# GpSimd adds up the residual between the scatters of two pairs, with x loaded in eight pieces ahead of the loop

## What is computed

```
xn = _layernorm(x)                       # x: (8, 1024, 128) = 64 tiles of 128 tokens
out = x + mamba2(xn) + moe(xn)           # mamba2(xn) itself returns xn + y @ W_out.T

# mamba2: y is scaled row by row with rsqrt(mean(y*y) + eps) ahead of W_out
# moe: the two best of 8 experts for each token, weights w from a softmax
h   = silu(xn @ gate[e]) * (xn @ up[e])  # 128 -> 256
moe = sum over the token's two experts of w * (h @ down[e])
```

## Time and profile before

| | us |
|---|---|
| median of 3 runs | 794.11 (792.69 to 797.33) |
| the profiled execution's own time | 795.79 |
| its span, first to last instruction | 794.0 |
| PE busy | 631.2 (79%) |
| DVE busy | 585.2 (74%) |
| ACT busy | 462.3 (58%) |
| POOL busy | 400.4 (50%) |
| first scatter to `moe_d` starts | 520.12 |
| first final load is issued | 760.32 |

### The profile page before, as it was taken

The page is one execution under the profiler, slowest core; times in us unless marked ns, Lnnn a source line. Parts: engine busy times, 40 slices in busy tenths (PEclk is TensorE's granted clock), DMA queues, the critical chain, the costliest instruction groups (busy, mean ns, idle before and its releaser), DMA issues. The chain is left out here.

```text
span 794.0 us, 15139 instructions
## 1 busy us (share of the span) xinstructions
PE 631.2 (79%) x3701; PEld 531.9 (67%) x3703; DVE 585.2 (74%) x1410; ACT 462.3 (58%) x1014; POOL 400.4 (50%) x601
## 2 busy tenths in 40 slices
PE   0695629998999989999998998699898889988700
PEld 0695317777778777778777776587777777777600
DVE  7787898898898888888898888555565555654445
ACT  0352446688777878877788775454555555554400
POOL 3000006576766766766676767145555555555510
PEclk9999999799999999999999999799999999999955
DMA  9950100000000000000000015133333333333169
GB/s 306 266 130 0 29 1 23 19 27 23 29 22 22 28 22 22 28 22 22 25 26 22 29 24 184 36 88 99 97 85 96 88 98 98 85 98 86 54 252 382
DMA packets 64647, 61.43 MB, mean 77 GB/s; under 512 B 9242, under 2 KB 55710, under 8 KB 64624
## 3 DMA queue, kind: packets, MB, share of 16 engines
q1 hardware_dynamic: 56176, 44.11, 19.7%
q0 software_dynamic: 8448, 17.06, 6.2%
HBM read 30.19 MB, written 31.47 MB: 78 GB/s over the span
## 5 line engine op out<-in xcount | busy, mean ns | idle before, releaser
L449 POOL DMA_INDIRECT moe_d<-raw,slot_st x136 | 133.8, 984 | 124.6 <-issue 102.1
L422 POOL DMA_INDIRECT slots_d<-rows,slot_st x128 | 134.6, 1052 | 73.8 <-POOL rows L417 52.5
L1040 DVE SCALAR_TENSOR_TENSOR act<-raw,taps,act 128x512 f32<-128x512 f32 x192 | 149.3, 785 | 23.9 <-ACT act L513 23.1
L398 POOL TENSOR_TENSOR xde<-xb,e_end 128x256 f32<-128x256 f32 x64 | 45.6, 713 | 113.2 <-DVE xb L1117 111.6
L1233 DVE CAST x_hi<-bank 128x256 fp32r<-128x256 f32 x68 | 28.8, 424 | 95.4 <-PE bank L871 91.8
L864 PE MATMUL bank<-xw_hi,x_hi 128*128 x136 | 61.1, 449 | 27.2 <-DVE x_lo L1235 22.7
L774 PE MATMUL bank<-xb,m_sb 128*128 128x64 f32 x512 | 75.9, 298 | 3.8 <-POOL xde L398 3.8
L774 PEld LDWEIGHTS bank<-xb,m_sb 128*128 128x128 f32 x512 | 73.1, 216 | 5.6 <-issue 3.9
L890 PE MATMUL bank<-act,raw 128*128 x544 | 72.0, 275 | 1.8 <-issue 1.8
L664 ACT ACTIVATE raw<-bank 128x256 f32<-128x256 f32 x68 | 26.5, 391 | 77.2 <-remote 68.5
L890 PEld LDWEIGHTS bank<-act,raw 128*128 128x128 f32 x544 | 66.1, 192 | 1.9 <-issue 1.9
(11 more groups left out here) (231 smaller groups left out, 1659.4 us busy)
## 6 DMA issues: line engine op xcount, KB each, us to landing
slots_d<-rows SPq DMA_DIRECT2D x8, 1122.0 KB, 13.4
rows<-slots_d SPq DMA_DIRECT2D x68, 132.0 KB
x_sb<-in_x SPq DMA_DIRECT2D x8, 512.0 KB, 7.0
act<-in_x SPq DMA_DIRECT2D x64, 64.0 KB
xw_hi<-moe_d SPq DMA_DIRECT2D x8, 512.0 KB, 9.3
xw_lo<-moe_d SPq DMA_DIRECT2D x8, 512.0 KB, 9.9
out<-x_sb SPq DMA_DIRECT2D x8, 512.0 KB, 13.5
moe_d<-raw,slot_st POOLq DMA_INDIRECT x136
```

What stands on the lines that cost most here:

```text
L398: nc.gpsimd.tensor_tensor(by_head(xde[:, u, :]), by_head(xdt[:, u, :]), per_head(e_end, nn), ALU.mult).then_inc(xde_done, 1)
L422: nc.gpsimd.indirect_dma_start(out=slots_d, out_offset=bass.IndirectOffsetOnAxis(ap=slot_st[:, r, c:c + 1], axis=0), in_=rows[:, r, c, :], ...
L449: nc.gpsimd.indirect_dma_start(out=moe_d, out_offset=bass.IndirectOffsetOnAxis(ap=slot_st[:, r, c:c + 1], axis=0), in_=ym[r][:, c * D:(c + ...
L1040: V.scalar_tensor_tensor(out=group_act(par)[:, t, :], in0=proj[:, t, k:k + GT], scalar=taps[:, t, k:k + 1], in1=group_act(par)[:, t, :], o ...
```

## The change

An internal HBM tensor `x_d` is added, and SP copies x to it (4 MB, HBM to HBM) behind the writes that clear `slots_d`. The eight x loads go from `x_d` to `x_again`, which now is a region of `xw_lo` (64 tiles, 4 MB), behind the first weights. So the low part of the gate and up weights moves to the second half of `xw_hi`. The 64 loads of the pair loop are gone. ACT reads `x_again[:, t]` and writes `x_norm[r]`, which has the place of the old `x_again[r]`. The multiply-add of DVE becomes a multiply and an add on POOL, behind the two scatters of its step, and a semaphore `resid_added` takes the place of `place_free`.

```
-        gu_hi, gu_lo = xw_hi[:, 0:E * 2 * F], xw_lo[:, 0:E * 2 * F]
+        gu_hi, gu_lo = xw_hi[:, 0:E * 2 * F], xw_hi[:, E * 2 * F:2 * E * 2 * F]
-        x_again = [act[:, 3072 + r * D:3072 + (r + 1) * D] for r in range(R)]
+        x_again = xw_lo[:, 0:NT * D].bitcast(F32).rearrange("p (t d) -> p t d", d=D)
+        x_norm = [act[:, 3072 + r * D:3072 + (r + 1) * D] for r in range(R)]
...
@@ sync
+            sp.dma_start(x_d, x).then_inc(st_x, 16)
             sp.wait_ge(csp_done, 4)
...
             gate_up_load(raw[:, 0:3072], 0, 6, ld_moe_w)
+            sp.wait_ge(st_x, 16)
+            sp.wait_ge(proj_done, NG * NAT)
+            for i in range(8):
+                sp.dma_start(x_again[:, 8 * i:8 * i + 8, :], x_d[:, 8 * i:8 * i + 8, :]).then_inc(ld_again, 16)
             sp.wait_ge(gate_done, NT - GC)
             gate_up_load(act[:, 0:1024], 6, 2, ld_moe_w2)
...
-            def load_again(m, r):
-                sp.wait_ge(place_free, m * R + r + 1)
-                sp.dma_start(x_again[r], x[:, tile_ix(m * R + r), :].rearrange("p a d -> p (a d)"))\
-                    .then_inc(ld_again[r], 16)
-            sp.sem_inc(place_free, R)
-            over_pairs(sp, [(slot_load, 0)], [load_again])
+            over_pairs(sp, [(slot_load, 0)])
+            sp.wait_ge(resid_added, NT)
...
@@ gpsimd
+            def residual(m, r):
+                t = tile_ix(m * R + r)
+                xt = x_sb[:, t, :].rearrange("p a d -> p (a d)")
+                pool.wait_ge(rms_done, 1)
+                pool.wait_ge(resid_done, m * R + r + 1)
+                pool.sem_inc(scatters, 1)
+                nc.gpsimd.tensor_tensor(xt, xt, var[:, t].broadcast_to([P, D]), ALU.mult).then_inc(resid_scaled, 1)
+                pool.wait_ge(resid_scaled, m * R + r + 1)
+                pool.sem_inc(scatters, 1)
+                nc.gpsimd.tensor_tensor(xt, xt, x_norm[r], ALU.add)\
+                    .then_inc(resid_added, 1)
-            over_pairs(pool, [(moe_scatter, 0)])
+            over_pairs(pool, [(moe_scatter, 0)], [residual])
...
@@ scalar
                 act_e.wait_ge(rms_done, 1)
-                act_e.wait_ge(ld_again[r], 16 * (m + 1))
+                act_e.wait_ge(ld_again, 16 * 8)
                 t = tile_ix(m * R + r)
-                A(x_again[r], x_again[r], ACT.Identity, bias=nmr1[:, t], scale=r12[:, t]).then_inc(resid_done, 1)
+                if not is_first(m):
+                    act_e.wait_ge(resid_added, (m - 1) * R + r + 1)
+                A(x_norm[r], x_again[:, t, :].rearrange("p a d -> p (a d)"), ACT.Identity, bias=nmr1[:, t],
+                  scale=r12[:, t]).then_inc(resid_done, 1)
...
@@ vector
-            def residual(m, r):
-                dve.wait_ge(resid_done, m * R + r + 1)
-                t = tile_ix(m * R + r)
-                xt = x_sb[:, t, :].rearrange("p a d -> p (a d)")
-                V.scalar_tensor_tensor(out=xt, in0=xt, scalar=var[:, t], in1=x_again[r], op0=ALU.mult, op1=ALU.add)\
-                    .then_inc(place_free, 1)
-            over_pairs(dve, [(x_keep, 0), (destination, 2), (hidden, 1)], [residual])
+            over_pairs(dve, [(x_keep, 0), (destination, 2), (hidden, 1)])
-            dve.wait_ge(place_free, NT + R)
+            dve.wait_ge(resid_added, NT)
```

More of the change, by code:

```diff
@@ L77, in program @@
         ncs_d = nc.dram_tensor("ncs_d", (2 * NH, NT, P), F32, kind="Internal").ap()
+        x_d = nc.dram_tensor("x_d", (P, NT, D), F32, kind="Internal").ap()
         x_sb = sb("x_sb", [P, NT, D])
@@ L174, in program @@
             "ld_w", "ld_moe_w", "ld_moe_w2", "st_zero", "st_cs", "st_out"))
-        scatters = sem("scatters")
+        scatters, st_x = sem("scatters"), sem("st_x")
         ld_x = [sem(f"ld_x{i}") for i in range(8)]
@@ L180, in program @@
         st_moe = [sem(f"st_moe{i}") for i in range(R)]
-        ld_again = [sem(f"ld_again{i}") for i in range(R)]
+        ld_again = sem("ld_again")
         ld_sum = [[sem(f"ld_sum{i}_{c}") for c in range(K)] for i in range(8)]
@@ L208, in program @@
         gu_hi_done, gu_lo_done, xhi_done = sem("gu_hi_done"), sem("gu_lo_done"), sem("xhi_done")
-        ms_done, rms_sq, rms_done, resid_done, place_free, total_done = (sem(n) for n in (
-            "ms_done", "rms_sq", "rms_done", "resid_done", "place_free", "total_done"))
+        ms_done, rms_sq, rms_done, resid_done, resid_added, total_done = (sem(n) for n in (
+            "ms_done", "rms_sq", "rms_done", "resid_done", "resid_added", "total_done"))
+        resid_scaled = sem("resid_scaled")
         def by_head(t):
```

## The result

| | before | changed |
|---|---|---|
| median, us | 795.01 (792.69 to 797.33, 4 runs) | 907.51 (903.7 to 908.14, 4 runs) |
| ratio | | 1.139, 95% interval 1.136 to 1.143 |
| profiled execution's own time / span | 795.79 / 794.0 | 908.12 / 906.4 |
| first scatter starts | 520.12 | 525.81 |
| scatter of pair 4 | 535.15 | 540.12 |

The rows of before in the second half of the table are those of the earlier trace rows and of the table ahead. The span grew by 112.4 us: 5.0 up to pair 4, 103.2 from pair 4 to pair 63, 4.2 from there to the last scatter, nothing behind it.

What follows compares the result with a forecast made beforehand. PE alone is not the limit; POOL's groups of four scatters and late `y_keep` repeat, 3.53 us a step. The new wait's ring adds 94 us, the loads 2: 892 from the profiled 795.79, so 890 as median, range 868 to 922.

Steps and rivals of the forecast that it cites:

- the ring: Pair loop: `y_keep`, scatters, multiply, add and ACT's residual run one after another, 5.08 us a step against 3.53; +94.1 us.
- the two POOL operations: POOL's multiply and add behind each pair's scatters: 0.38 us each, bounds 0.30 and 0.60.
- ACT's idle time: Pair loop: ACT idle 2.5 to 3 us before its residual in each step, released by POOL's add.
- The tail: Pairs 65 to 67, where ACT has no residual: they follow as fast as POOL can, 3.67 us each.
- rival 2: Pair loop: the ring does not bind, POOL's own work does; 3.67 us a step, 804 us; chance 0.06.
- the 0.83: Pair loop: part of the time from the add's start to the next scatter, taken as 1.23 less `y_keep`'s own time.
- The copy: Before the pair loop: copying x to `x_d` costs 0 to 10 us, taken as 0.
- The +2 for the loads: Before the pair loop: x loads delay the last weights, ACT waits 0 to 5 us, taken as +2.
- Rival 3: Pair loop: POOL operations break up four scatters holding `y_keep` back; no slower or faster, 782 to 784 us; chance 0.04.
- the hold on `y_keep`: Pair loop before the change: `y_keep` starts only 0.99 us after the last of four scatters; what holds it not shown.

Runs made afterwards that it cites:

- e1: Changed kernel with eight `x_norm` places in place of four, so ACT waits for the add eight tiles back: 827.83 us against 792.25 before (1.046).
- e3: Changed kernel with POOL's multiply and add put ahead of the scatters of each step, four places kept: 818.86 us against 792.25 before (1.034).
- The doses: Changed kernel without POOL's multiply (866.04 and 864.42 us) or with its add done twice (942.25 us); one execution each.
- e7: Changed kernel with POOL's multiply by the row factor left out: 866.04 us in one execution, where the kernel before takes 765.15.
- e12: Kernel before plus one unused 128x128 POOL add behind each step's two scatters, on a slow-kind chip: 798.05 us against 795.89 (1.001).
- e4: Kernel before plus a one-column POOL memset that nobody reads, behind each step's two scatters: 795.63 us against 792.25 (1.010).
- e5: Kernel before plus one unused 128x128 POOL add behind each step's two scatters, on the fast chip: 767.43 us against 765.15 (1.000).
- e6: Changed kernel with the fused multiply-add back on DVE and the eight x loads behind the last weight loads: 766.49 us against 765.15 before (1.0006).
- e10: Same kernel as e5 (kernel before plus an unused 128x128 POOL add), run again on the fast chip: 766.11 us against 764.86 (1.001).
- e9: The changed kernel itself, run again where the kernel before takes 764.86 us: 904.45 us (1.180).
- e2: Changed kernel with the fused multiply-add back on DVE, which frees the place; copy, loads and moved weights stay: 795.35 us against 792.25 before (1.004).

## Why the prediction was right, point by point

**The forecast** of 890 (868 to 922) named the ring, and the ring is what happened; the measured 907.51 lies in the range and 17.5 over the value.

**The ring.** e1 and e3 remove it, one by more places and one by the order of the queue, and with it 77 and 86 of the 112 us, each against the kernel before of its own group. The doses move the step by what they add or take. That is shown. Its terms, against the earlier trace rows:

| term | predicted | measured in the rows above |
|---|---|---|
| `y_keep` to first scatter | 1.23 | 1.20 |
| two scatters, to the multiply | 2.27 + 0.02 | 610.82 - 608.53 = 2.29 |
| multiply | 0.38 | 0.44 |
| multiply to add | 0.17 | 0.19 |
| add | 0.38 | 0.46 |
| add to ACT's residual | 0.25 | 612.16 - 611.91 = 0.25 |
| residual to `y_keep` | 0.38 | 0.40 |
| sum | 5.08 | 5.23 |

The term that was mis-sized is the two POOL operations, 0.14 of the 0.15 us: halving the variable part of the 0.60 us of the earlier trace rows gave 0.38, and they take 0.44 and 0.46. The rule of the Trainium skill (GPSIMD Engine Reference, section 4.1) that such work takes GpSimd about twice as long as VectorE would have made each 0.69; the trace has 1.3 times the 0.347 us of the earlier trace rows for each, and two operations stand in place of one fused. So the rule was too high here for one operation. ACT's idle time, which I gave as 2.5 to 3 us, is 3.44: it is the 5.23 of the ring less the 1.79 from the residual at 606.93 to the end of ACT's last copy at 608.72, and I had not worked it out.

**Where the 17.5 us are.** 60 x (5.23 - 5.08) = 9.0. The first step of a turn takes 0.13 more, 14 times: 1.8. One step, from pair 56 to 57, takes 7.07 in place of 5.24: 1.8. The second scatter of pair 56 starts 3.14 us behind the first, where it is at most 1.32 in all other pairs, and this is so in all 14 profiles, that of before among them. No term of the forecast had it, and its cause is open. Up to pair 4 it was 5.0, not 2.0: 3.0. The tail has 3.81 a step and not 3.67, 0.4. Sum 16.0. Of the 1.5 that are left about 1.1 is how the two profiled executions stand to their medians (1.7 above in the prediction, 0.6 here).

**The tail.** 3.67 was the sum for a step bound by POOL alone, in the tail and in rival 2. It is 3.82, and again the two operations are what was too small: multiply 0.43, add 0.45 to 0.46. From the end of the add to the next scatter it is 0.45 us in the tail, exactly the 0.83 less 0.38 of the prediction. That was luck in part: the 0.83 came from a step in which the scatter waits for `y_keep`, while in e7 and e12 it follows its one operation after 0.17.

**The front.** The copy cost nothing: the issue to `cs_d` that the earlier trace rows has at 84.76 now starts at 84.59. The +2 for the loads was about right as a mean. The first scatter starts at 520.3 to 525.8, mean 523.5, in the eight profiles with the loads ahead of the weights, and at 520.1 to 522.3, mean 521.2, in the six others (before, e4, e5, e6, e10, e12). The mechanism I gave for it, weights that land late, is only part: ACT waits 1.1 to 1.4 us for them ahead of its last conversion in six of the eight and in none of the six others, but in the changed kernel's first profile and in e3 it doesn't wait at all. In the first profile of the changed kernel, the one of the result, TensorE's granted clock is down to 0.74 while the loads run; in e9, the same program, it stays at 1.00 there, and the first scatter comes 4.9 us earlier (525.81 and 520.89):

```profile
470.00:490.00 20.00, 18.83 (x100) 15.87 (x98) 13.99 (x35) 11.44 (x25) 13.40 (x26) 0.74 0.74 277
```

The columns are as above, and this is the same window of e9:

```profile
470.00:490.00 20.00, 17.71 (x121) 14.89 (x120) 17.69 (x38) 13.11 (x29) 15.44 (x27) 1.00 0.78 284
```

Both have issued the first weights at nearly the same time (474.83 and 474.50), so the two executions part behind that. The last 1.8 us of the 4.9 come behind the first gate product, which starts at 512.34 and 509.19. Here is the changed kernel's first profile and then e9:

```profile
508.00:525.00 17.00, 12.54 (x48) 9.52 (x48) 6.82 (x19) 6.71 (x14) 0.00 (x0) 0.60 0.08 20
...
508.00:525.00 17.00, 14.13 (x78) 11.77 (x79) 8.49 (x25) 7.14 (x18) 2.97 (x3) 0.88 0.13 33
```

So one and the same program differs by 4.9 us in this place, and the slower execution has the lower clock. That doesn't make the 5.0 us the clock alone. In e1 the clock is 1.00 from 470 to 490 and the first scatter still comes at 525.38. And a clock below 1.00 from 470 to 490 is seen only in two of the eight profiles with the loads ahead of the weights (here and in e3, 0.66), in none of the six others, so the loads may have a part in it. How the 5.0 us divide is open.

**PE.** It waits 2.07 us ahead of L899 in the step shown, as forecast, but 1.4 us as a mean of all steps: (215 - 157.48) us over the 41 steps of the window. Its clock did fall, to a mean of 0.90, so that in some steps its work takes longer (the down products above 1.44 us and not 1.06). It did not reach the ring: the sum of the ring's terms, in which no PE instruction stands, is the whole step.

**Rival 2** (bound by POOL, 804) is what e1 and e3 made; it costs more than the 804 said, by the 3.82 for 3.67 and the time that the front takes. **Rival 3** (POOL's work breaks the hold on `y_keep`) is refuted by e12: an operation stands between the pairs and the hold stays. The prediction left open what the hold is, and that stays open. It is not the 64 loads (e2), an operation of 0.43 us between the pairs does not end it (e12), and it is not in the program alone, since the same program has it in some groups and not in others. The ring of the changed kernel does not contain it, hence nearly the same 904 and 908 us in both kinds. It shows only before the ring begins: from the first scatter to pair 4 it is 14.31 us in the changed kernel's first profile and 11.72 in e9, 2.6 us apart. From pair 4 to pair 63 it is 312.41 and 312.46.

## What to carry to other kernels

Before a new wait is added to an in-order queue, write down which step of the other queue it refers to, what that step stands behind, and what stands behind the waiting instruction; if that closes a ring within one step, its latencies add up, whatever the busy shares say. POOL and ACT were both about half idle here, and the change cost 14%. The cure is a place more or another order (e3 moves two instructions and gives back 86 of 112 us), and only after that does the work's own size count.

## What the runs showed of the hardware

The kernel before takes 792 to 796 us in three groups of runs and 765 in two, 4% apart. Both groups of 765 us are of one chip. The profiles put the difference in the pair loop: `y_keep` starts late in every second pair (idle of 2.5 to 2.7 us, put down to "remote") in the one kind, and never does in the other, 3.55 against 3.11 us a step in the same program (e12, e5). A ratio measured in one kind (1.14) isn't that of the other (1.18).

A scatter's instruction on POOL takes 0.98 us, 1.00 to 1.01 when it is the first behind other work, with 0.30 to the next. A 128x128 multiply or add takes 0.43 to 0.46, in e7 up to 0.51, a step from one to the next through a semaphore mostly 0.18 to 0.19 (0.26 to 0.32 in e1). A scatter whose own waits are met starts 0.17 behind a single operation (e7, e12) and 0.44 behind a multiply and an add (e3). From `y_keep`'s end to the scatter that it releases it is 608.53 - (607.33 + 0.36) = 0.84 us, far more than the 0.25 from POOL's add to ACT.
